# GpSimd also waits for every output transfer before it leaves its program

## The chip, the core and the metric

The kernel runs on one core of one Trainium2 chip. The metric is the device time of one execution of the whole program, in microseconds (us). A core has five engines, each with an instruction stream of its own: TensorE (PE), VectorE (DVE), ScalarE (ACT), GpSimd (POOL) and SyncE (SP). [...]
## The reference

One decoder layer on `x` of 32 x 128 x 128 in float32: causal linear attention with 16 heads, windowed cross attention on a context, and a mixture of 8 experts with top-1 routing, each with a residual and a layer norm behind it.

```python
x = _layernorm(x + _L0_attn_ref(x, L0_attn_qkv_w, L0_attn_qkv_b, L0_attn_out_w, L0_attn_out_b), axis=-1)
x = _layernorm(x + _L0_xattn_ref(x, ctx_1024, ctx_1024, L0_xattn_W_proj, L0_xattn_b_proj), axis=-1)
x = _layernorm(x + _L0_ffn_ref(x, L0_ffn_wg, L0_ffn_W1, L0_ffn_b1, L0_ffn_W2, L0_ffn_b2), axis=-1)
```

Inside the experts, `capacity = int(N / E * 1.25) + 1 = 641` rows are held for each of the 8 experts; a token beyond that is passed on without an expert.

## The kernel before

The program is written by hand, engine by engine, in one block. Each engine's stream is a function (`@block.sync`, `@block.gpsimd`, and so on), and the order of the work on an engine is the order in which its function writes it; nothing is scheduled by a tool. All waits are written out as `wait_ge` on a semaphore.

The first three quarters of the time go over the 32 sequences, 128 tokens each: both attentions, the router, and then `op_scatter`, which lays the sequence's rows into the experts' buffer in DRAM. That is 32 indirect DMAs issued by GpSimd on line 498. SyncE stores a fallback row for every token in `out` (line 338).

The rest goes over the 8 experts. Each expert's rows are loaded by SyncE, go through two layers on TensorE, and VectorE adds the residual and normalises them into the tiles `ot`. GpSimd writes each finished tile of 128 rows to the tokens' places in `out` with an indirect DMA (`scatter`, line 641, 40 of them). The 641st row of each expert is carried along apart, and these 8 rows are written last, by `scatter_rest` on line 648. GpSimd's DMAs are raised on five semaphores: the 40 on `out_done[0]` to `out_done[3]` in turn by group of tiles, the last one on `rest_out`.

SyncE's stream ends with waits for all of them, lines 405 to 407:

```python
            for k in range(4):
                sp.wait_ge(out_done[k], 16 * sum(len(GROUPS[n][1]) for n in range(k, len(GROUPS), 4)))
            sp.wait_ge(rest_out, 16)
```

GpSimd's stream ends with the issue of `scatter_rest()`, line 665. When the block is left, every engine runs a DRAIN, an instruction of the sequencer, and then a barrier of all five engines: GpSimd collects a count from the four others and releases them. All of this is shown under line 80, on which the context that holds the block is opened; line 2410 is the same at the start of the program, where the launcher begins it.

Of the kernel before, what the change touches and what calls it, by code (L numbers as in the profile page):

```python
# [47 lines left out]
def decoder(nc, x, ctx_in, qkv_w, qkv_b, out_w, out_b, proj_w, proj_b, wg, W1, b1, W2, b2, out):  # L48
    B, T, D = x.shape
    E, _, F = W1.shape  # L50
    HD = 8
    H = D // HD
# [27 lines left out]
    with ctx:  # L80
# [6 lines left out]
        def sem(name):  # L87
            return ctx.enter_context(nc.semaphore(name))

        banks = ctx.enter_context(nc.psum_tensor("banks", [P, 8, 512], F32))  # L90
        BANKS = {name: used for name, _, used in JOBS}

        def bank(name):
# [137 lines left out]
        GROUPS = [(e, tiles) for e in range(E) for tiles in ([[0, 1], [2, 3, 4]] if e < E - 1 else [[0], [1, 2], [3, 4]])]  # L231
# [71 lines left out]
        out_done = [sem(f"out_done{k}") for k in range(4)]  # L303

        er_in, rest_full, var_rest, root_ready = sem("er_in"), sem("rest_full"), sem("var_rest"), sem("root_ready")
        ot_rest, rest_out = sem("ot_rest"), sem("rest_out")
# [103 lines left out]
        def _(pool):  # L410
# [224 lines left out]
            def scatter(n, which):  # L635
                e, tiles = GROUPS[n]
                pool.wait_ge(idx_ready, e + 1)
                for t in which:
                    c = tiles[t]
                    pool.wait_ge(ot_ready, e * ET + c + 1)  # L640
                    g.indirect_dma_start(out=out.rearrange("b t d -> (b t) d"),  # L641
                                         out_offset=bass.IndirectOffsetOnAxis(ap=idx[e % 3][:, c:c + 1], axis=0),
                                         in_=ot[n % 4][:, t, :], in_offset=None, bounds_check=N - 1,
                                         oob_is_err=False).then_inc(out_done[n % 4], 16)

            def scatter_rest():
                pool.wait_ge(ot_rest, 1)
                g.indirect_dma_start(out=out.rearrange("b t d -> (b t) d"),
                                     out_offset=bass.IndirectOffsetOnAxis(ap=idxr[:], axis=0),
                                     in_=otr[:], in_offset=None, bounds_check=N - 1,  # L650
                                     oob_is_err=False).then_inc(rest_out, 16)
# [11 lines left out]
            scatter(second, [0, 1])  # L663
            scatter(third, [0, 1])
            scatter_rest()

        @block.tensor
        def _(pe):
# [1752 lines left out]
```

## Time and profile before

| what | us |
|---|---|
| median of 3 runs | 431.02 (429.87 to 433.3) |
| the profiled execution | 431.97 |
| its span, from the first to the last instruction | 430.2 |
| outside the span | 1.77 |

The rows below are of that one profiled execution, and its times count from the start of the span. A chain of waits is followed back from the last instruction, and a row of it is the stretch for which that engine held the end up. A row of a source line gives, for each operation on the line, the count, the shortest, median and longest duration in nanoseconds, and when the first and the last of them started, to a tenth of a microsecond.

### The profile page before, as it was taken

Reading aid. Unit: us, or ns where it says so; the run is one execution under the profiler, and the core shown is the slowest. Engines: PE = TensorE matmul, PEld = TensorE weight load, DVE = VectorE, ACT = ScalarE, POOL = GpSimd, SP = SyncE. Lnnn points to the kernel's source line nnn. Section 1 sums busy time; section 2 is a strip of 40 time slices with the busy share of each in tenths; the row PEclk is TensorE's granted clock in tenths of the full one; section 3 lists DMA queues with packets and bytes.
Section 4 is the critical chain, followed back from the end, with each engine's and each line's share of the span. In section 5 each row is a group of like instructions: output and inputs, shape, how many; then the busy total and the mean of one; then the engine's idle time right before and its main releaser. Section 6 shows DMA issues by size and latency. Waiting matters only on the chain.

```text
span 430.2 us, 19219 instructions
## 1 busy us (share of the span) xinstructions
PE 401.2 (93%) x7097; PEld 298.2 (69%) x7097; DVE 331.8 (77%) x1640; ACT 267.2 (62%) x603; POOL 252.3 (59%) x372
## 2 busy tenths in 40 slices
PE   6999999999999999999999999998888999999960
PEld 5657676777677677777677767776676788888850
DVE  6367688888788888788888898888876487887772
ACT  4755767777777777777777777865546434444420
POOL 5253454566666676666566866666545057677653
PEclk9999999999999999999999999999999999999995
DMA  4910000101101011110111122010021333343100
GB/s 112 317 38 17 15 16 15 28 28 47 29 26 29 28 34 39 36 29 26 28 34 29 39 64 79 21 28 15 17 59 35 102 101 118 112 134 114 32 26 16
DMA packets 25859, 22.74 MB, mean 53 GB/s; under 512 B 3623, under 2 KB 21090, under 8 KB 25766
## 3 DMA queue, kind: packets, MB, share of 16 engines
q1 hardware_dynamic: 23430, 17.30, 13.6%
q0 software_dynamic: 2336, 4.20, 3.1%
q8 instruction: 58, 0.95, 0.9%
q14 instruction: 35, 0.29, 0.2%
HBM read 12.46 MB, written 9.58 MB: 51 GB/s over the span
## 4 chain that ended last, share of the span: by engine, by line
PE 74%; ACT 8%; DVE 8%; issue 5%; POOL 1%; DMA 1%; POOLq 0%; SPq 0%; DVEq 0%; ACTq 0%
PE banks L772 14%; PE banks L722 13%; PE banks L714 8%; PE banks L1222 8%; ACT arena L1508 8%; PE banks L734 7%; PE banks L707 6%; PE banks L784 4%; PE banks L851 2%; PE banks L752 2%; PE banks L800 1%; PE banks L1202 1%; PE banks L753 1%; PE banks L754 1%; PE banks L823 1%
## 5 line engine op out<-in xcount | busy, mean ns | idle before, releaser
L1681 DVE TENSOR_REDUCE mx<-banks 128x8 f32<-128x1024 f32 x64 | 75.6, 1219 | 33.7 <-PE banks L722 33.6
L1247 ACT ACTIVATE arena<-banks 128x1024 f32<-128x1024 f32 x64 | 62.3, 1022 | 31.7 <-PE banks L722 31.7
L772 PEld LDWEIGHTS banks<-arena,V 128*32 128x32 f32 x2048 | 53.1, 109 | 29.9 <-ACT arena L1277 23.4
L1277 ACT ACTIVATE arena<-banks 128x1024 f32<-128x1024 f32 x64 | 62.2, 1021 | 16.7 <-PE banks L714 16.5
L772 PE MATMUL banks<-arena,V 128*32 128x128 f32 x2048 | 67.2, 275 | 0.3 <-ACT arena L1277 0.2
L1508 ACT ACTIVATE arena<-banks,b1T 128x321 f32<-128x321 f32 x64 | 33.8, 529 | 42.1 <-PE banks L1202 41.5
L641 POOL DMA_INDIRECT out_x<-ot,idx x40 | 40.2, 1006 | 23.1 <-DVE ot L2331 14.7
L482 POOL TENSOR_TENSOR rs<-ve,minus_half 128x2 f32<-128x2 f32 x32 | 23.2, 725 | 52.1 <-DVE ve L1669 52.0
L498 POOL DMA_INDIRECT expert_in<-x,sidx x32 | 35.1, 1097 | 14.1 <-DVE x L1755 6.0
L459 POOL TENSOR_TENSOR QE<-qT,head_mask 128x512 f32<-128x512 f32 x32 | 33.1, 1034 | 16.4 <-DVE qT L1592 16.2
L1265 ACT ACTIVATE CE<-banks,head_mask 128x128 f32<-128x128 f32 x128 | 36.6, 371 | 9.7 <-PE banks L707 9.5
L465 POOL TENSOR_TENSOR rs<-ve,minus_half 128x1 f32<-128x1 f32 x32 | 18.0, 563 | 41.5 <-DVE ve L1649 41.5
L1222 PE MATMUL banks<-w_sb,arena 128*128 128x128 f32 x320 | 38.1, 278 | 0.0
L1222 PEld LDWEIGHTS banks<-w_sb,arena 128*128 128x128 f32 x320 | 36.4, 192 | 1.6 <-issue 1.6
L1202 PE MATMUL banks<-arena,w_sb 128*128 128x320 f32 (+1 forms) x128 | 36.1, 433 | 0.0
L722 PE MATMUL banks<-QE,kT 32*128 32x512 f32 x256 | 36.1, 635 | 0.1
L714 PE MATMUL banks<-x1T,CE 32*128 32x128 f32 x1024 | 36.0, 277 | 0.0
L722 PE MATMUL banks<-CE,x1T 32*128 32x512 f32 x256 | 35.2, 617 | 0.0
L714 PEld LDWEIGHTS banks<-x1T,CE 32*128 32x128 f32 x1024 | 31.6, 187 | 0.0
L1202 PEld LDWEIGHTS banks<-arena,w_sb 128*128 128x128 f32 x128 | 23.6, 190 | 9.6 <-DVE arena L2247 0.6
L489 POOL TENSOR_SCALAR x<-r,mv,rs 128x128 f32<-128x128 f32 x32 | 25.5, 797 | 7.1 <-DMA expert_in<-x,sidx 6.7
L471 POOL TENSOR_SCALAR x<-r,mv,rs 128x128 f32<-128x128 f32 x32 | 25.5, 797 | 2.6
(207 smaller groups left out, 967.6 us busy)
## 6 DMA issues: line engine op xcount, KB each, us to landing
w_sb<-in_L_ffn_W SPq DMA_DIRECT2D x16, 256.0 KB, 3.1
EB<-expert_in SPq DMA_DIRECT2D x9, 325.0 KB, 4.0
expert_in<-zeros SPq DMA_DIRECT2D x10, 266.5 KB, 3.3
X<-in_x SPq DMA_DIRECT2D x32, 64.0 KB, 1.8
C<-in_ctx SPq DMA_DIRECT2D x32, 64.0 KB, 2.0
out_x<-fb SPq DMA_DIRECT2D x32, 64.0 KB, 1.6
out_x<-ot,idx POOLq DMA_INDIRECT x40, 2.2
b2b<-in_L_ffn_b SPq DMA_DIRECT2D x1, 512.0 KB
```

The lines of the kernel that those rows point to most:

```text
L498: g.indirect_dma_start(out=buf, out_offset=bass.IndirectOffsetOnAxis(ap=sidx[b % 4][:], axis=0), in_=x2[b % 4][:], in_offset=None, bounds_ ...
L641: g.indirect_dma_start(out=out.rearrange("b t d -> (b t) d"), out_offset=bass.IndirectOffsetOnAxis(ap=idx[e % 3][:, c:c + 1], axis=0), in_ ...
L714: mm = pe.matmul(banks[:, used, a * P:(a + 1) * P], weights(part, a), moved(part, a), start=False, stop=last and a == NA - 1, tile_positio ...
L722: mm = pe.matmul(banks[:, used, :], weights[part, :], moved[part, :, :].rearrange("p a t -> p (a t)"), start=False, stop=True, tile_positi ...
L772: mm = pe.matmul(bank(name)[VW * s:VW * (s + 1), half * P:(half + 1) * P], V[:, h, :], scored[:, h // NA, h % NA, :], start=q == 0, stop=q ...
L1202: pe.matmul(act_bank[j % 4][:, 0:r1 - r0], w1_sb[e % 2][:, f * P:(f + 1) * P], ebT[e % 2][:, r0:r1], start=True, stop=True).then_inc(h_ful ...
L1222: mm = pe.matmul(y_bank[k][:, 0:D], hT[e % 2][:, f, (k - 1) * P:k * P], w2_sb[e % 2][:, f, :], start=(f == 0), stop=(f == FC - 1))
L1247: nc.scalar.activation(A1[b % 2][:, 2 * half:2 * half + 2].rearrange("p j a t -> p j (a t)"), pair("s1", half), ACT.Relu).then_inc(s1_out[ ...
L1265: last = nc.scalar.activation(CE[b % 4][:, a, :], bank("cT")[:, 0:P], ACT.Copy, scale=head_mask[:, a:a + 1])
L1277: nc.scalar.activation(P2[b % 2][:, 2 * half:2 * half + 2].rearrange("p j a t -> p j (a t)"), pair("s2t", half), ACT.Exp, scale=SCALE).the ...
L1508: nc.scalar.activation(hT[e % 2][:, f, r0:r1], act_bank[j % 4][:, 0:r1 - r0], ACT.Gelu, bias=b1T[:, e * FC + f:e * FC + f + 1]).then_inc(h ...
L1681: v.tensor_reduce(mx[b % 2][:, 8 * half:8 * half + 8].rearrange("p (j a) -> p j a", a=NA), pair("s2", half).rearrange("p j (a t) -> p j a ...
```

## The change

Three lines are added at the end of GpSimd's stream, behind the issue of the last DMA. They wait for the same five semaphores, with the same values, as SyncE's waits, which stay. No instruction of any other engine differs, and nothing is queued on GpSimd behind the new waits but its DRAIN and its part of the barrier.

```diff
@@ -663,6 +663,9 @@
             scatter(second, [0, 1])
             scatter(third, [0, 1])
             scatter_rest()
+            for k in range(4):
+                pool.wait_ge(out_done[k], 16 * sum(len(GROUPS[n][1]) for n in range(k, len(GROUPS), 4)))
+            pool.wait_ge(rest_out, 16)
 
         @block.tensor
```

## Rows read from the trace of the kernel before

**Rows 1.** The page: the span, and TensorE's and GpSimd's busy time

```profile
span 430.2 us, 19219 instructions
...
PE 401.2 (93%) x7097; PEld 298.2 (69%) x7097; DVE 331.8 (77%) x1640; ACT 267.2 (62%) x603; POOL 252.3 (59%) x372
```

**Rows 2.** The chain of waits from 421.75 us to the end: start us, us, what

```profile
421.75 0.47 POOL out_x L641
422.22 0.59 issue
422.81 1.15 POOLq L80
```

**Rows 3.** Source line 80: the way out of the block, all engines

```profile
L80 POOLq EVENT_SEMAPHORE  x2: 17/17/17, 430.1 to 430.1; - x2
L80 PEldq DRAIN  x1: 1940/1940/1940, 414.8 to 414.8; - x1
L80 ACTq DRAIN  x1: 231/231/231, 420.9 to 420.9; - x1
L80 DVEq DRAIN  x1: 376/376/376, 421.8 to 421.8; - x1
L80 POOLq DRAIN  x1: 7200/7200/7200, 422.8 to 422.8; - x1
L80 SPq COMPARE_BRANCH  x1: 38/38/38, 425.1 to 425.1; - x1
L80 SPq DRAIN  x1: 7/7/7, 425.3 to 425.3; - x1
L80 SPq EVENT_SEMAPHORE  x1: 17/17/17, 430.2 to 430.2; - x1
```

**Rows 4.** Timeline from 422 us: the last work of VectorE and GpSimd

```profile
421.75 0.97 POOL L641 DMA_INDIRECT out_x<-ot,idx  x1 [0.30 <-issue]
421.82 0.34 DVE L2396 TENSOR_SCALAR otr<-r3r,mvr,rsr 8x128 f32<-8x128 f32 x1
423.06 0.90 POOL L648 DMA_INDIRECT out_x<-otr,idxr  x1 [0.35 <-issue]
```

**Rows 5.** Source line 407: SyncE's wait for the last output transfer

```profile
L407 SPq EVENT_SEMAPHORE  x1: 28/28/28, 425.1 to 425.1; - x1
```

**Rows 6.** Source line 648: the last DMA, from issue to landing

```profile
DMA to landing us min/median/max: 2.0/2.0/2.0
```

**Rows 7.** Waits of SyncE's queue: waited for, us in total, times, longest

```profile
SPq L80 <- PEq L80: 4.9, 1, 4.9
SPq L407 <- DMA out_x<-otr,idxr: 3.8, 1, 3.8
```

**Rows 8.** Busy time in stretches of the end: PE, PEld, DVE, ACT, POOL, clock, DMA

```profile
422.80:424.00 1.20, 0.00 (x0) 0.00 (x0) 0.00 (x0) 0.00 (x0) 0.90 (x1) 0.50 0.14 47
424.00:425.10 1.10, 0.00 (x0) 0.00 (x0) 0.00 (x0) 0.00 (x0) 0.00 (x0) 0.50 0.01 1
425.10:430.20 5.10, 0.00 (x0) 0.00 (x0) 0.00 (x0) 0.00 (x0) 0.00 (x0) 0.50 0.00 0
```

**Rows 9.** Source line 2410: DRAINs at the start of the program, before any DMA

```profile
L2410 SPq DRAIN  x1: 7/7/7, 0.0 to 0.0; - x1
L2410 DVEq DRAIN  x1: 10/10/10, 0.1 to 0.1; - x1
...
L2410 PEldq DRAIN  x1: 8/8/8, 0.3 to 0.3; - x1
...
L2410 POOLq DRAIN  x1: 174/174/174, 0.4 to 0.4; - x1
L2410 POOL MEMSET const-uint8-127<- x1: 102/102/102, 0.4 to 0.4; 128x1 uint8 x1
```

**Rows 10.** Source line 498: GpSimd's indirect DMAs into the experts' buffer

```profile
L498 POOL DMA_INDIRECT expert_in<-x,sidx x32: 969/1112/1244, 86.7 to 332.6; - x32
```

**Rows 11.** Source line 641: GpSimd's indirect DMAs of the finished tiles

```profile
L641 POOL DMA_INDIRECT out_x<-ot,idx x40: 966/974/1126, 348.2 to 421.7; - x40
```

## The prediction, written before the changed kernel was run

> **What bounds the kernel now.** I read the views from the outside in. The page first: TensorE is busy for 401.2 of 430.2 us [rows 1], so nearly all of the time is TensorE's and the stages that feed it, and nothing of that is touched. The change sits behind the last instruction that GpSimd issues, so what counts is the end of the span, and I read that in four views.
>
> The chain of waits ends in GpSimd: its last tile store, an issue, and then its sequencer on line 80 from 422.81 us [rows 2]. The chain shows only 1.15 us of that last row, up to 423.96, but the span goes on to 430.2. The row of the source line says what the rest is: GpSimd's DRAIN on the way out of the block takes 7,200 ns, from 422.81 to 430.01, and only then come its two barrier instructions, at 430.1, and the release of the others, at 430.2 [rows 2, 3]. The other engines are at their DRAIN much earlier: TensorE at 414.8, ScalarE at 420.9, VectorE at 421.8, SyncE at 425.3, and SyncE then waits 4.9 us at the barrier [rows 3, 7]. So the last 4.9 us of the kernel belong to GpSimd's DRAIN alone. In that time no engine works and no DMA engine moves anything [rows 8].
>
> What the DRAIN may be waiting for is seen beside it. GpSimd's last instruction, the indirect DMA of the odd rows, runs from 423.06 for 0.90 us, to 423.96 [rows 4]. Its data lands 2.0 us after it started, at 425.1, which is also when SyncE passes its last wait [rows 5, 6]. The DRAIN ends 6.05 us after the former and 4.9 us after the latter. It is waiting for neither alone.
>
> **The change part by part.** It removes nothing and moves nothing. It adds waits for five semaphores in front of GpSimd's DRAIN.
>
> The waits as instructions: SyncE has the same five. The one on line 407 takes 28 ns and the branch behind it 38 ns, and its DRAIN starts at 425.3, about 0.2 us after the landing at 425.1 [rows 3, 5]. GpSimd would pass its own by the same events, since the last of them, the landing, is the same one; its DRAIN then starts at 425.3 instead of 422.81, 2.5 us later. That delay by itself is not on the end's path, since the path is where the DRAIN ends, and that depends on how long it takes when it starts after all transfers have landed. Nothing else is queued behind the new waits. Those who wait for GpSimd are the four other engines at the barrier, the latest of them there at 425.3 [rows 3], so whatever the DRAIN takes after that is the kernel's.
>
> The price of a late DRAIN is not in this trace, so I bound it from both sides. The lower bound is the DRAIN of GpSimd at the start of the program, before it had issued any DMA: 174 ns, with a 102 ns memset in flight beside it [rows 9]. The upper bound is the 7,200 ns that it took here [rows 3]. In between are two readings of the same row. If the DRAIN's work begins once GpSimd's last DMA instruction has left the engine, it is 430.01 - 423.96 = 6.05 us of work. If it ends a fixed time after the last landing, that is 430.01 - 425.1 = 4.9 us.
>
> I take 6.05 us. The reason is the difference between the two DRAINs of the same engine: 174 ns with nothing issued before it, and over 6 us with 32 + 40 + 1 = 73 indirect DMAs issued [rows 4, 9 to 11]. Those DMAs cost GpSimd 0.9 to 1.24 us each, with medians of 974 and 1,112 ns and no long one among them [rows 4, 10, 11], so nothing in the run shows GpSimd taking stock of the transfers that are done; if something does, it is the DRAIN. Such a stock-taking goes over 73 entries (83 ns each, by 6.05 / 73) or over the 16 DMA engines (0.38 us each), and either is work that has to be done whether the transfers have landed or not. Of 73 transfers at most two were still open when it began: the last tile store started at 421.75 and the odd rows at 423.06, at some 2 us to land [rows 4, 6]. Work that begins at 425.3 in place of 423.96 ends 1.34 us later: 431.35 in place of 430.01. The sum is **+1.3 us**, 431.97 + 1.3 = 433.3 for an execution like the profiled one. That one lies 0.95 us over the median of the three runs; against the median the same sum gives 431.02 + 1.3 = **432.3 us**.
>
> The only end of the program that has a DRAIN of any length is GpSimd's. SyncE's took 7 ns, and those of VectorE and ScalarE, 376 and 231 ns, cover an instruction that was still running: VectorE's last one started at 421.82 for 0.34 us [rows 3, 4]. At the start of the program SyncE, VectorE and TensorE have 7 to 10 ns [rows 9].
>
> [...]
>
> **The rivals.**
>
> First, *the end follows the last landing*. The DRAIN goes over the transfers, is held by the one that is still open, and needs 4.9 us from there. Then its end does not care when it began, as long as that is near the landing: from 425.1 it ends where it did, from 425.3 it ends at 430.2. That is 0 to +0.2 us, 431.0 to 431.2. For it speaks that the transfer open longest lands inside the DRAIN; against it that nothing moves in the 4.9 us behind the landing [rows 8].
>
> Second, *the 7.2 us are a wait badly done*: the DRAIN looks for open transfers, finds one at 423.96, and looks again only much later. With all of them landed it would pass at the first look, at the 174 ns of the start of the program: 425.3 + 0.17 = 425.5, 4.5 us earlier, 426.5 us. For it: the long DRAIN is the one with transfers open and the short one had none [rows 3, 9], and the 4.9 us of nothing behind the landing fit an idle pause [rows 8]. Against it: a pause of this length for transfers that take 2 us to land [rows 6]. [...]
>
> Third, on the other side, *the whole 7.2 us start anew*. The sequencer's DRAIN begins at 422.81, 0.25 us before the last DMA instruction starts on the engine [rows 3, 4]. If its work runs in the sequencer from there and not behind the engine, then none of the 7,200 ns is cover for the DMA instruction, and the late start of 2.5 us is paid in full: 425.3 + 7.2 = 432.5, +2.5 us, 433.5 us. It decides from the point where nothing in the DRAIN's work depends on the engine being done. Against it: the DRAINs of VectorE and ScalarE plainly wait for their engine's last instruction.
>
> That the change does nothing at all I leave out as a case of its own: SyncE's wait for the same landing is passed only at 425.1, so GpSimd's cannot be passed before it.
>
> **How the numbers follow.** The forecast (work of 6.05 us, +1.3) has a chance of 0.36; the end tied to the landing (0 to +0.2) 0.30; the pause that goes away (-4.5) 0.22; the whole anew (+2.5) 0.12. For this kernel about 1% is what a measurement can tell from no change: three runs lie between 429.87 and 433.3. The pause that goes away gives -4.5 of 431.02, 1.04%, so it is over the line in a little more than half of its cases: 0.12 faster. The rest are all within 1%, but for 0.03 that the runs' own scatter carries the slower ones over it: 0.85 within. The range has to reach to the pause, since 0.22 is more than may be left out: from 426.0, which is its 426.5 less half a microsecond of scatter, to 434.5, which is the 433.5 of the slower rival and a microsecond of scatter. The likeliest case has 431.0 to 433.7 for its own.
>
> **What would show it.** In the profile of the changed kernel GpSimd's DRAIN on line 80 should start at 425.3 and take about 6.0 us; 4.9 us would be the first rival, under 0.4 us the second, 7.2 the third. SyncE's wait at the barrier, 4.9 us now, should grow to about 6.2. Everything up to 423 us should be as it was. The prediction is wrong if the DRAIN's length follows open transfers rather than the number of DMAs behind it, or if the time before 423 us moves, for which I see no reason.

## The result, and the profile after

The changed kernel took 433.20 us (median of 9 runs, 432.85 to 435.05) against 431.78 us (median of 9 runs, 429.87 to 433.3) for the kernel before. The ratio is 1.0042, with a 95% interval from 1.0026 to 1.0059: slower by 1.8 us, between 1.1 and 2.5 us; the two medians lie 1.4 us apart. Forecast were +1.3 us and no change that goes over 1%.

The page of the changed kernel, its span and its busy times, beside [rows 1]:

```profile
span 432.1 us, 19222 instructions
...
PE 400.8 (93%) x7097; PEld 297.8 (69%) x7097; DVE 332.2 (77%) x1640; ACT 267.2 (62%) x603; POOL 252.8 (58%) x372
```

Three instructions more (of the five new waits two have a row in the trace, on lines 667 and 668, and the third is GpSimd's branch on line 80), and every engine's busy time within 0.5 us of what it was. Source line 80 of the changed kernel, the way out of the block, beside [rows 3] (count, shortest, median and longest in ns, first and last start in us):

```profile
L80 POOLq EVENT_SEMAPHORE  x2: 17/17/17, 431.9 to 432.0; - x2
...
L80 DVEq DRAIN  x1: 376/376/376, 422.3 to 422.3; - x1
L80 SPq COMPARE_BRANCH  x1: 38/38/38, 425.7 to 425.7; - x1
L80 POOLq COMPARE_BRANCH  x1: 38/38/38, 425.7 to 425.7; - x1
L80 SPq DRAIN  x1: 7/7/7, 425.8 to 425.8; - x1
L80 POOLq DRAIN  x1: 6039/6039/6039, 425.8 to 425.8; - x1
```

SyncE and GpSimd now pass the same events at the same time and come to their DRAINs together, at 425.8. SyncE's takes 7 ns, GpSimd's 6,039 ns. Before, GpSimd's began 2.5 us before SyncE's and took 7,200 ns [rows 3]. The new wait that is passed last, on line 668 of the changed kernel:

```profile
L668 POOLq EVENT_SEMAPHORE  x1: 43/43/43, 425.6 to 425.6; - x1
```

The timeline of the changed kernel has GpSimd's last DMA, beside [rows 4]:

```profile
423.57 0.90 POOL L648 DMA_INDIRECT out_x<-otr,idxr  x1 [0.34 <-issue]
```

It ends at 424.47 here and at 423.96 before, so the profiled execution came to this place 0.51 us later, ahead of the change; the nine runs of the kernel before differ among themselves by up to 3.4 us, and the 0.51 is not put down to the change. From there the DRAIN ends 7.4 us later (431.9), and 6.05 us before: 1.4 us that are the change's. The rest of the 1.9 us between the two spans is the 0.51. SyncE's wait at the barrier, among the waits of its queue, beside [rows 7]:

```profile
SPq L80 <- PEq L80: 6.2, 1, 6.2
```

It grew from 4.9 to 6.2 us.

The barrier itself can be read from the semaphore operands and their increments in the trace of the kernel before. The DRAINs of TensorE, ScalarE, VectorE and SyncE each add one to the same semaphore, at 416.73, 421.10, 422.22 and 425.32, within 0.02 us of each DRAIN's end. GpSimd's first instruction behind its own DRAIN, at 430.05, waits for that semaphore and takes from it; its second, at 430.14, adds to another. The last instruction of each of the four others, at 430.18 to 430.19, waits for this other one and takes one from it. SyncE's is in [rows 3]; those of the other three are

```profile
L80 ACTq EVENT_SEMAPHORE  x1: 17/17/17, 430.2 to 430.2; - x1
L80 DVEq EVENT_SEMAPHORE  x1: 21/21/21, 430.2 to 430.2; - x1
L80 PEldq EVENT_SEMAPHORE  x1: 51/51/51, 430.2 to 430.2; - x1
```

In the changed kernel GpSimd's two are at 431.93 and 432.01 and the others' at 432.05 to 432.06. At the start of the program, on line 2410 of the kernel before, the same instructions stand at 0.60, 0.68 and 0.72 to 0.73.

### The profile page after: what moved, and what is told of

Same layout as the page of the kernel before. It is cut to its first block, busy times and chain, and to the rows that moved or that the text cites. A ratio compares the mean times of both kernels' runs of the same rounds, so it can differ in the third digit from the quotient of the medians.

```text
span 432.1 us, 19222 instructions
## 1 busy us (share of the span) xinstructions
PE 400.8 (93%) x7097; PEld 297.8 (69%) x7097; DVE 332.2 (77%) x1640; ACT 267.2 (62%) x603; POOL 252.8 (58%) x372
## 4 chain that ended last, share of the span: by engine, by line
PE 72%; DVE 10%; ACT 8%; issue 5%; POOL 2%; DMA 1%; POOLq 0%; DVEq 0%; SPq 0%; ACTq 0%
PE banks L775 14%; PE banks L725 13%; PE banks L717 8%; PE banks L1225 8%; ACT arena L1511 8%; PE banks L737 7%; PE banks L710 6%; PE banks L787 4%; PE banks L854 2%; PE banks L755 1%; PE banks L803 1%; DVE y1T L1761 1%; PE banks L1205 1%; PE banks L826 1%; DVE mxs L1701 1%
```

## The experiments

The forecast says that GpSimd's DRAIN is work that begins when nothing is left ahead of it. It left two things open: whether that work goes over the DMAs or over something fixed, and whether the DRAIN also waits for transfers that are still open.

**A DRAIN held back further.** The changed kernel, with four memsets on GpSimd behind the new waits, into a tile `idle` that nothing else uses.

```diff
             pool.wait_ge(rest_out, 16)
+            for _ in range(4):
+                g.memset(idle[:], 0.0).then_inc(consts, 1)
+                CONSTS_NOW.append(1)
+                pool.wait_ge(consts, CONSTS + len(CONSTS_NOW))
```

> The changed kernel with four memsets of 128 x 1024 on GpSimd behind the new waits, which hold the DRAIN back by some microseconds more. Theory (work that begins when the DRAIN begins): the DRAIN takes 6.04 us again and the end moves by all that the memsets take. Rival 2 (an end tied to the landing): the DRAIN gets shorter by what the memsets take, and the end stays. No theory but this one has a pause left in the DRAIN: if it were a look that comes round at fixed times, its length would differ from 6.04 us by up to that period.

The timeline and line 80 of that kernel:

```profile
424.89 3.98 POOL L672 MEMSET idle<- 128x1024 f32 x4 [1.23 <-DMA out_x<-otr,idxr]
```

```profile
L80 POOLq DRAIN  x1: 6039/6039/6039, 429.1 to 429.1; - x1
```

6,039 ns to the nanosecond, although it began 4.3 us behind the last landing (424.76, the last of the 16 increments that this DMA's semaphore has in the trace, the first being at 424.56). The kernel was run once, in 437.07 us. The end is not tied to the landing, and a look that comes round at fixed times, which would change the length with the start, does not show.

**Two DRAINs ahead of the expert stage.** The kernel before, with

```diff
+            pool.drain()
+            pool.drain()
             for k in range(2):
                 pool.wait_ge(fb_out[k], 16 * (B // 2))
```

> The kernel before, with two DRAINs of GpSimd one behind the other after its 32 indirect DMAs of line 498 and before the expert stage, where GpSimd sits idle from 333.6 to 346.2 us. Theory (the DRAIN goes over every indirect DMA issued since the last DRAIN, 6.04 / 73 = 83 ns each): the first takes 32 x 83 ns = 2.6 us, the second under 0.2 us, and the last one, over 41, 3.4 us behind the last DMA instruction: the end comes 2.6 us earlier, ratio 0.994. Rival 1 (a fixed cost of every DRAIN once DMAs are in use, such as one look at each of 16 engines): 6 us, 6 us and 7.2 us, time unchanged or up to 1 us later. Rival 2 (it goes over all DMAs of the program again at each DRAIN): 2.6, 2.6 and 7.2 us, time unchanged.

The DRAINs on their lines, and GpSimd's timeline around the first:

```profile
L653 POOLq DRAIN  x1: 3892/3892/3892, 331.8 to 331.8; - x1
...
L654 POOLq DRAIN  x1: 41/41/41, 335.7 to 335.7; - x1
...
L80 POOLq DRAIN  x1: 4566/4566/4566, 422.3 to 422.3; - x1
```

```profile
332.04 0.97 POOL L498 DMA_INDIRECT expert_in<-x,sidx  x1 [3.79 <-DVE x L1757]
345.65 0.72 POOL L632 TENSOR_TENSOR rs<-ve,minus_half 128x2 f32<-128x2 f32 x1 [12.64 <-DVE ve L2304]
...
422.51 0.90 POOL L648 DMA_INDIRECT out_x<-otr,idxr  x1 [0.34 <-issue]
```

The first ends at 335.71, 2.70 us behind the DMA that it was queued on (333.01), with 32 DMAs issued since the start. The second has none and takes 41 ns. The last ends at 426.82, 3.41 us behind its DMA (423.41), with 41. A fixed cost of each DRAIN falls, and so does one over all DMAs of the program. GpSimd's wait of 12.64 us ahead of the expert stage is as long as in the kernel before (12.6 us): the two DRAINs cost nothing there. The ratio to the kernel before is 0.9908 (0.9878 to 0.9938, five runs), a larger gain than the 0.994 that was expected, which lies just outside that interval. The next kernel has one DRAIN there and twelve runs.

**One DRAIN there.**

> The kernel before with a single DRAIN of GpSimd ahead of the expert stage, in its 12.6 us of idle time. Theory (83 ns for each DMA of 128 rows since the last DRAIN, and no end before the last landing): 2.7 us behind the last DMA of line 498 there, 3.4 us behind the last DMA at the end in place of 6.05; the end comes 2.65 us earlier, ratio 0.994. Rival (there was a further gain in the run with two of them, whose ratio was 0.991): 0.991 again.

Ratio 0.995 (0.993 to 0.997), 429.36 us. The DRAIN at the end is again

```profile
L80 POOLq DRAIN  x1: 4566/4566/4566, 422.5 to 422.5; - x1
```

which is 3.41 us behind the last DMA, as with two DRAINs. What the two had beyond 0.994 did not come back; the second of them took 41 ns, and I take the rest for scatter.

**A DRAIN in every expert.** To the single DRAIN ahead of the expert stage are added

```diff
                 root(2 * e)
+                pool.drain()
                 scatter(2 * e, [0])
...
             scatter(first, [0])
+            pool.drain()
             scatter(second, [0, 1])
```

> The kernel before, with a DRAIN of GpSimd ahead of the expert stage, one in each expert behind the root of its first group, where GpSimd waits for VectorE for 1.2 to 1.9 us, and one behind the first tile store of the last expert, where it waits 1.9 us. Theory (83 ns for each DMA since the last DRAIN): 2.6 us for the first, 0.1 to 0.4 us for those in the experts unless a transfer is still open, and 5 x 83 = 0.4 us for the last; it ends at the last landing, 425.1, or little after it, about 4.5 us earlier than before, ratio 0.990. Rival (fixed cost of 6 us for each DRAIN): GpSimd is late in every expert, 7 x 4 us or more, ratio 1.06 or more. Rival (all DMAs again each time): 2.6 us rising to 6 us, ratio 1.03 or more.

The ratio is 0.9994 (0.9966 to 1.0023): neither the gain nor a loss of several per cent. The DRAINs in the experts, and GpSimd's timeline around the second of them:

```profile
L658 POOLq DRAIN  x7: 821/3812/4296, 347.2 to 408.5; - x7
```

```profile
355.40 0.97 POOL L641 DMA_INDIRECT out_x<-ot,idx  x1 [0.30 <-issue]
356.38 0.74 POOL L632 TENSOR_TENSOR rs<-ve,minus_half 128x2 f32<-128x2 f32 x1
359.83 1.03 POOL L641 DMA_INDIRECT out_x<-ot,idx  x1 [2.71 <-issue]
```

That DRAIN begins at 355.13 and ends at 358.95, with 5 DMAs to go over, when GpSimd has been idle since 357.12. By the semaphore's increments in the trace the store of 355.40 landed at 358.70. The DRAINs in the five later experts end the same 0.24 to 0.25 us behind the last landing each time, though those landings lie 1.2 to 2.8 us behind the end of the last store's instruction, and so does the one at the end of this kernel. The one behind the last expert's first store ends 0.28 us behind that store's landing. So a DRAIN of GpSimd does wait for open transfers, which my theory named only as an exception. The store that follows starts 0.88 us after the DRAIN, and the rows of GpSimd's sequencer in between are that store's waits and register moves (lines 640 and 641, from 358.99 to 359.73): its issue is prepared only behind the DRAIN. GpSimd is late in every expert, and that eats what the end gains. Its last DMA and its last DRAIN:

```profile
427.96 0.91 POOL L648 DMA_INDIRECT out_x<-otr,idxr  x1 [0.30 <-issue]
```

```profile
L80 POOLq DRAIN  x1: 3565/3565/3565, 426.6 to 426.6; - x1
```

The last DMA starts 4.9 us later than in the kernel before (423.06), and the DRAIN, with its end at 430.2, ends no earlier than there (430.01).

**Two DRAINs, or three, where GpSimd has time.** With one ahead of the expert stage and one in the last expert:

> The same, and a second DRAIN behind the first tile store of the last expert (GpSimd idle there from 415.8 to 417.8 us). Theory: the second goes over 36 DMAs, 3.0 us, so the next store starts 1.1 us late and the last lands at about 426.2; the DRAIN at the end has 5 DMAs left, 0.4 us, and ends 0.25 us behind that landing: 3.5 us earlier than before, ratio 0.992. Rival (a cost of each DRAIN that is not the DMAs' count): no gain over a single one, 0.994.

Ratio 0.995 (0.993 to 0.997), as with one alone: a miss by 0.003. The second DRAIN, and the timeline of GpSimd:

```profile
L664 POOLq DRAIN  x1: 4196/4196/4196, 415.9 to 415.9; - x1
```

```profile
416.13 0.97 POOL L641 DMA_INDIRECT out_x<-ot,idx  x1 [1.23 <-DVE ot L2333]
420.97 0.99 POOL L641 DMA_INDIRECT out_x<-ot,idx  x1 [3.87 <-DVE ot L2333]
```

The DRAIN ran for 4,196 ns from 415.91 to 420.10, 3.00 us behind the first of these stores, as expected for 36 DMAs. But the next store started another 0.87 us later. I had counted the whole idle time as room for a DRAIN; the last 0.8 us of it (416.95 to 417.77 in the kernel before) are the sequencer's preparation of the next DMA, and here they came behind the DRAIN. With a third DRAIN, in the fifth expert:

```diff
                 root(2 * e)
+                if e == 4:
+                    pool.drain()
                 scatter(2 * e, [0])
```

> The same, and a third DRAIN in the fifth expert behind the root of its first group. Theory: that one waits for the transfer still open and holds the next store back by some 1.4 us, which the slack of the ot tiles may take up; the one in the last expert then has 16 DMAs, 1.3 us, inside the idle time, and the end is the last landing and 0.25 us: 4.7 us earlier than before if the 1.4 us are taken up, ratio 0.989, and 3.3 us earlier if not, 0.992.

Ratio 0.9907 (0.9881 to 0.9933, six runs), 427.48 us: between the two, and the shortest of these versions. By the ratio alone it can't be told from the kernel with two DRAINs; the profile tells them apart, since the DRAIN at the end ends 2.23 us behind the start of the last DMA here, and 4.31 us there. Its DRAINs, and the last stores:

```profile
L659 POOLq DRAIN  x1: 2477/2477/2477, 383.2 to 383.2; - x1
...
L666 POOLq DRAIN  x1: 3132/3132/3132, 414.1 to 414.1; - x1
...
L80 POOLq DRAIN  x1: 3102/3102/3102, 422.3 to 422.3; - x1
```

```profile
414.34 0.97 POOL L641 DMA_INDIRECT out_x<-ot,idx  x1 [1.24 <-DVE ot L2335]
418.12 0.97 POOL L641 DMA_INDIRECT out_x<-ot,idx  x1 [2.82 <-issue]
...
423.21 0.90 POOL L648 DMA_INDIRECT out_x<-otr,idxr  x1 [0.30 <-issue]
```

The DRAIN at the end has 5 DMAs and ends at 425.44, 0.24 us behind the last landing (2.0 us after 423.21). The one in the fifth expert did not end by an open transfer, as the theory had it: the last landing was at 384.26, 1.37 us before its end. Counted from the store ahead of it, it made the next store 0.7 us late against the kernel with one DRAIN (4.46 us in place of 3.75), but the sixth expert's first store is on time again (13.77 and 13.78 us), so this one cost nothing. The one in the last expert had 16 DMAs, which is 1.3 us, and took 1.95 us behind its DMA, in this kernel and in the next one. The landing doesn't account for that either: it came at 416.56, 0.69 us before the DRAIN's end at 417.25. That 0.6 us isn't explained. The next store starts 0.87 us behind the DRAIN, and, counted from the store ahead of it, 0.9 us later than in the kernel with one DRAIN; at the last DMA 0.7 us of that are left, and so much is missing from the 4.7 us of the theory.

**The same, with the changed kernel's waits.**

> The kernel with DRAINs ahead of the experts, in the fifth and in the last, and the changed kernel's waits at the end. Theory: the last DRAIN has 5 DMAs, 0.45 us, which without the waits are hidden while the last transfer is under way, and which start behind its landing with them: landing + 0.25 + 0.45 us in place of landing + 0.25, some 0.45 us later than without the waits, ratio to before 0.992 in place of 0.991. Rival (the waits cost 1.3 us whatever is left to go over): 0.994.

Ratio 0.9911 (0.9878 to 0.9943); the intervals of this and the kernel without the waits overlap nearly whole, and the rival's 0.994 lies in this one, so the profile decides. Line 80 of this kernel and its last DMA:

```profile
L80 SPq DRAIN  x1: 7/7/7, 427.9 to 427.9; - x1
L80 POOLq DRAIN  x1: 455/455/455, 427.9 to 427.9; - x1
```

```profile
425.59 0.91 POOL L648 DMA_INDIRECT out_x<-otr,idxr  x1 [0.31 <-issue]
```

455 ns, the 0.45 that was expected for 5 DMAs. The last DMA landed at 427.6, and the DRAIN ends 0.73 us behind that in place of 0.24. The same waits that cost 1.4 us over 73 DMAs cost 0.5 us over 5.

**More DMAs ahead of the DRAIN.** The changed kernel with more indirect DMAs into a scratch buffer behind the new waits, each waited for: 64 of 8 rows, 64 of 128 rows, and then 32 and 128 of 8 rows. The diff is that of the first, with arguments left out (`...`) and without the buffer's own line, by which line 80 becomes line 81.

```diff
             pool.wait_ge(rest_out, 16)
+            for n in range(64):
+                g.indirect_dma_start(out=dump, ..., in_=otr[:], ...).then_inc(dumped, 16)
+                pool.wait_ge(dumped, 16 * (n + 1))
```

> The changed kernel with 64 more indirect DMAs of the 8 odd rows into a scratch buffer in DRAM, one after the other behind the new waits, each waited for; its time is longer for them by some 64 x 3 us, and only the length of the DRAIN is read. Theory (83 ns for each DMA): 137 x 83 ns = 11.3 us. Rival 1 (a fixed cost): 6.0 us. Rival 3 (the cost goes with the rows written, 9,224 of them and 512 more): 6.4 us.

> The changed kernel with 64 more indirect DMAs behind the new waits as in the run with 64 small ones, but of 128 rows each. That run's DRAIN took 8.9 us, 45 ns for each DMA of 8 rows. Theory A (the cost of a DMA goes with its descriptors: 45 ns for 8 rows, 83 ns for 128): 6.04 + 64 x 83 ns = 11.4 us. Theory B (what the DRAIN goes over is bounded, at some 107 DMAs): 8.9 us again.

> The changed kernel with 32 more indirect DMAs of 8 rows behind the new waits; only the length of the DRAIN is read. By now DRAINs over 36, 41 and 73 DMAs took 3.00, 3.41 and 6.04 us behind the last DMA, and 137 took 8.90 us whether small or full. If what the DRAIN goes over is bounded near 107, the 105 DMAs here still cost 82 ns each: 8.7 us. If it is cheaper from the 74th on, 45 ns each: 7.5 us.

> The same with 128 more, 201 in all. Bounded: 8.9 us as with 137. Cheaper from the 74th on: 6.04 + 128 x 45 ns = 11.8 us.

The DRAIN in these four (64 small, 64 full, 32 and 128 small):

```profile
L81 POOLq DRAIN  x1: 8897/8897/8897, 601.1 to 601.1; - x1
```

```profile
L81 POOLq DRAIN  x1: 8897/8897/8897, 620.1 to 620.1; - x1
```

```profile
L81 POOLq DRAIN  x1: 8652/8652/8652, 514.5 to 514.5; - x1
```

```profile
L81 POOLq DRAIN  x1: 10531/10531/10531, 781.6 to 781.6; - x1
```

The size of a DMA doesn't matter: 64 of 8 rows and 64 of 128 rows give the same 8,897 ns. From 73 to 105 DMAs, all 32 of 8 rows, the DRAIN grows by 2,613 ns, 82 ns for each, which is also the price between 32 and 73 DMAs, nearly all of 128 rows. Up to 105 DMAs the count explains the length, but for the DRAIN with 16. Beyond that it doesn't: 137 took 8.9 us, not 11.3, and 201 took 10.5, neither the 8.9 of a bound nor the 11.8 of a constant lower price. In the run with 128 more the step from one DMA to the next is 0.8 to 0.9 us longer at the 129th and at the 161st DMA of the program, and in the runs with 64 more it is 0.8 us longer once, at the 129th (8 rows) or the 115th (128 rows); with 32 more no step is that long. What happens at those steps, and whether it has to do with a DRAIN of less than 82 ns for each DMA, stays open.

## Why the prediction was right

**The end.** That the last 4.9 us belonged to GpSimd's DRAIN, with all else done, held: a shorter DRAIN moved the end of the kernel by what it was shorter, and a later one by what it was later. The span ends 0.23 to 0.24 us behind the end of this DRAIN in all thirteen profiles. The prediction says that no DRAIN but GpSimd's has any length and leaves out TensorE's 1,940 ns [rows 3]; that one was over at 416.7, 0.1 us behind TensorE's last matmul, and cost nothing.

**The waits as instructions.** GpSimd's DRAIN was to begin about 0.2 us behind the landing, along with SyncE's. Both began at 425.8 behind waits passed at 425.6. A move of the time before 423 us was named as a sign of being wrong; the 0.51 us there is less than the runs of one kernel differ by, and the 1.4 us counted from the last DMA doesn't hold it.

**The price of the late DRAIN.** I took 6.05 us, between 0.17 and 7.2; it was 6,039 ns. The reason given for it, that the DRAIN goes over what was issued, was the right one of the two that I left side by side: it goes over the DMAs and not over the 16 DMA engines. The sum came out the same by either. The DRAINs over no more than 105 DMAs, whose end was not set by a landing, give the lengths below. They are counted from the end of GpSimd's last instruction, or from the start of the DRAIN where that is later (0, 5 and 105 DMAs, and 73 in the changed kernel).

| DMAs since the last DRAIN | us |
|---|---|
| 0 | 0.04 |
| 5 | 0.455 |
| 20 (fifth expert, best version) | 1.71 |
| 32 | 2.70 |
| 36 | 3.00 |
| 41 | 3.41 |
| 73 | 6.04 |
| 105 | 8.65 |

From 5 to 105 that is (8.652 - 0.455) / 100 = 82 ns for each DMA, and some 0.04 us besides; the forecast had 83. The one in the last expert of the best version, with 16 DMAs and 1.95 us, doesn't lie on this line.

**One clause was wrong and cost nothing.** I wrote of work "that has to be done whether the transfers have landed or not". The DRAIN also doesn't end before the last transfer has landed and 0.24 us more, as the run with a DRAIN in each expert shows. Here the 6 us over 73 DMAs hid that: for the landing's sake the DRAIN could have ended at 425.3 before, and after the change the last transfer had landed when it began.

**The rivals.** The end tied to the landing: a DRAIN is held by an open transfer, as this rival has it, but for 0.24 us behind the landing and not 4.9. The end came 4.9 us behind the landing before and 6.3 us after, and the DRAIN that was held back over 4 us kept its length. The pause that goes away: the DRAIN was 1.2 us shorter than before and not 7. All 7.2 us anew: 6,039 ns, so the first 1.15 us of the old DRAIN were cover for the DMA instruction in front of it.

**The sum.** +1.34 us stood against the 1.4 us between the DMA's end and the DRAIN's in the two profiled executions, and against 1.8 us (1.1 to 2.5) in the runs. The forecast of 432.3 us was put on the median of three runs; on the median of all nine runs of the kernel before the same sum is 433.1, and 433.2 was measured. So close a match is partly luck, since the runs tell the effect no better than 1.1 to 2.5 us.

## What to carry to other kernels

In these kernels GpSimd's DRAIN on the way out took 82 ns for each indirect DMA issued since the last DRAIN, up to 105 of them. So it should begin as early as it can: a wait in front of it moved that work behind the landing, which cost 1.4 us with 73 DMAs and 0.5 us with 5. A DRAIN of its own in an idle stretch in the middle of the program takes the count down for nothing (with one such DRAIN the kernel was 0.5% shorter, with three 0.9%), if no transfer is open there (where one was, the DRAIN ended 0.24 to 0.28 us behind its landing) and the idle time is more than the DRAIN plus the 0.9 us in which the sequencer prepared the next DMA. Time at the very end in which no engine is busy is still read from the trace: from the rows of the line that the block is left on.

## What was not expected of the hardware

- The length of GpSimd's DRAIN repeats to a few nanoseconds: 6,039 in two kernels, 4,566 in two, 8,897 in two, 3,890 to 3,892 in six.
- A DMA of 8 rows and one of 128 rows cost the DRAIN the same 82 ns.
- Beyond 105 DMAs the length grows more slowly and not evenly: 8.65 us for 105, 8.90 for 137, 10.53 for 201.
